# A position MLP whose y term is added once per two rows, and whose sums are stored every four rows

## The chip, the core and the metric

The kernel runs on one core of a Trainium2 chip. The metric is the device time of one execution in microseconds (us). Its engines are TensorE (PE; its weight loads are listed as PEld), VectorE (DVE), ScalarE (ACT), GpSimd (POOL) and SyncE (SP), which here only issues DMAs. Each has a queue of its own and they meet through semaphores. TensorE writes into PSUM, eight banks of 512 fp32 columns on 128 partitions.

## What is computed

The program is a chain of four attention-like layers. The change lies in the first one, a deformable attention, in the MLP that turns relative positions into a bias of the scores:

```python
pos  = grid_q[:, :, None, :] - grid_kv[:, None, :, :]     # 16 groups, 1024 queries, 64 keys, (x, y)
bias = sign(pos) * log1p(abs(pos))
bias = relu(bias @ cpb_w1 + cpb_b1)                       # 2 -> 128
bias = relu(bias @ cpb_w2 + cpb_b2)                       # 128 -> 128
bias = (bias @ cpb_w3 + cpb_b3)                           # 128 -> 1
sim  = q @ k^T + bias;  attn = softmax(sim);  out = attn @ v
```

That is 16 x 1024 x 64 = 1.05 million positions through a 128 x 128 layer.

## The kernel before

The program is a sequence of stages, each a block in which every engine has its own hand-written list of instructions; a block ends with a barrier. The bias stage, `stage_bias`, computes the whole MLP. It goes over 16 groups (bg) of 32 query rows (y), 512 rows in all; two rows are a pair, numbered i (256 pairs, n = i mod 16 within the group). A row has 32 x 64 = 2048 positions, that is four PSUM banks (q = 0 to 3).

- **Layer one** (DVE). The x part with bias and the y part of the hidden value are two tables of fp16 high and low words. DVE takes the maximum of the x table and one row of y values (line 888, 2.29 us a row) into `hw[i % 3]`, three buffers of a pair each, and counts `h1`. Since relu(x + y) = max(x, -y) + y, what is left is a term of y alone, which layer two adds.
- **Layer two** (TensorE). The y term is a product of 12 rows (bf16 pieces of y) with the y weights, line 851. For a row these are four matmuls on four row groups of the array, each into its own bank; they open the banks (start) and are called a y set here. Then for each bank three products in fp16 words (W2 high with low word, W2 low with high, W2 high with high), each as two matmuls of 64 columns side by side, line 862: 24 matmuls a row.
- **Relu** (ACT, line 927): each bank is read out, half of the hidden features into `tops[i % 3]`, half into `bots[i % 2]`, counted as `relu`.
- **Fold** (DVE, line 770): top + ratio x bottom for a pair, 2.35 us, so that layer three has one input instead of two. DVE folds pair i - 3 between the two h1 rows of pair i.
- **Layer three** (TensorE, line 764): for pair i four fp32 matmuls with 32 weight columns side by side, into the bank `p3`. The weight slice puts a pair's two rows in rows of their own, so 16 pairs add up in one bank. TensorE does two pairs of layer three behind every second pair: behind pair i (even) those of i - 2 and i - 1.
- **Copy and store**: once per group ACT adds the bias b3 and copies the bank (line 776), and SP stores it with 4 DMAs of 64 KB (line 781) to `bias_scratch` in DRAM.
- **Tables of the next group**: SP loads coordinates (line 166); ACT computes a value and its high word (lines 904 to 914), DVE the low word (line 874); four such jobs in a group.

The banks of layer two are a ring of seven; layer three has the eighth. At the stage's end SP issues eight loads of 256 KB (line 838), the bias of the first units of the attention stage. The attention stage starts with the last fold, copy and store of the bias stage.

Of the kernel before, what the change touches and what calls it, by code (L numbers as in the profile page):

```python
# [22 lines left out]
P = 128  # L23
# [195 lines left out]
def stage_front(K, sb, ps):  # L219
# [14 lines left out]
    small, x_in, zero = K.sem("small_loaded"), [K.sem(f"x_loaded{i}") for i in range(BLK)], K.sem("front_zeroed")  # L234
# [102 lines left out]
def stage_samples(K, sb, ps):  # L337
# [35 lines left out]
    nx_dram, nt_in, part = K.sem("nx_stored"), K.sem("nt_loaded"), K.sem("samples_step")  # L373
# [3 lines left out]
    cw_in, cw, w_mm, tab_out = K.sem("cpb_w_loaded"), K.sem("cpb_w_step"), K.sem("cpb_w_mm"), K.sem("tab_stored")  # L377
# [4 lines left out]
    with nc.Block() as block:  # L382
        @block.sync
        def _(sp):
            sp.dma_start(w2raw, d["cpb_w2"]).then_inc(cw_in, 16)
            sp.wait_ge(gelu_tanh, 2)
            for axis in range(2):
                for h in range(HALF):
                    sp.dma_start(dn[axis, :, h].unsqueeze(0), off[0:1, axis, h * BLK:(h + 1) * BLK]).then_inc(nx_dram, 16)
            sp.wait_ge(nx_dram, 16 * 2 * HALF)  # L390
            for r in range(QT):
                sp.dma_start(nt[r * n_ax:(r + 1) * n_ax, :], dn.rearrange("a k h j -> (a k h) j")).then_inc(nt_in, 16)
            sp.wait_ge(tab, 3)
            for axis in range(2):
                for r in range(QT):
                    at = r * n_ax + axis * BG
                    sp.dma_start(K.dl[axis, :, r * ROWQ:(r + 1) * ROWQ], pos[at:at + BG]).then_inc(tab_out, 16)
            sp.wait_ge(tab_out, 16 * 2 * QT)
            for job in range(2):
                T.load_coords(K, sp, T.co[job % 2], 0, job)  # L400
            sp.wait_ge(tab, 8)
            for r in range(QT):
                at = r * n_ax + BG
                sp.dma_start(K.dyp[:, :, r * ROWQ:(r + 1) * ROWQ].rearrange("g k y j -> g k (y j)"),
                             pieces[at:at + BG].rearrange("g k y j -> g k (y j)")).then_inc(pieces_out, 16)
            sp.wait_ge(pieces_out, 16 * QT)
            sp.wait_ge(T.ones, 1)
            T.load_y_rows(K, sp, T.rows, 0)
            for job in range(2, T.JOBS):
                sp.wait_ge(T.val_done, job - 1)  # L410
                T.load_coords(K, sp, T.co[job % 2], 0, job)

        @block.vector
        def _(dve):
# [20 lines left out]
            def weights_to_rows():  # L435
# [13 lines left out]
                dve.wait_ge(cw_in, 16)  # L449
# [252 lines left out]
def rings(n, banks):  # L702


    small = next(k for k in range(n) if (n - k * (banks - 1)) % banks == 0)
    at, spread = [], [banks] * ((n - small * (banks - 1)) // banks)
    for k in range(small):
        spread.insert((k * (len(spread) + 1)) // small, banks - 1)
    for size in spread:
        at += range(size)  # L710
    return at


def stage_bias(K, sb, ps):
# [18 lines left out]
    br = T.co[1][:, 0:BANK]  # L733
    banks = [ps(f"l2_ps{i}", [P, BANK]) for i in range(7)]
    p3 = ps("l3_ps", [P, BANK])
    PER = H * CH
    BANK_OF = rings(PER, len(banks))
    NROWS = BG * H

# [5 lines left out]
    def freed_by(row):  # L745
        least = 0
        for c in range(row * CH, row * CH + CH):
            before = [m for m in range(max(0, c - 2 * len(banks)), c) if BANK_OF[m % PER] == BANK_OF[c % PER]]
            if before:
                least = max(least, before[-1] + 1)  # L750
        return least
# [3 lines left out]
    folded, l3, copied, stored = K.sem("relu2_folded"), K.sem("l3_mm"), K.sem("rows_copied"), K.sem("rows_stored")  # L755

    def layer_three(pe, i):
        bg, n = divmod(i, PER_BG)
        pe.wait_ge(folded, i + 1)
        if bg and n == 0:  # L760
            pe.wait_ge(copied, bg)
        for q in range(CH):
            r, u = divmod(q, 2)
            last = nc.tensor.matmul(p3[32 * q:32 * q + 32, :], K.W3[:, 30 - 2 * n:62 - 2 * n], tops[i % 3][:, r, BANK * u:BANK * (u + 1)],  # L764
                                    start=(n == 0), stop=(n == PER_BG - 1), tile_position=(0, 32 * q))
        last.then_inc(l3, 1)
# [5 lines left out]
    def copy_rows(act, bg):  # L772
        act.wait_ge(l3, PER_BG * (bg + 1))
        if bg:
            act.wait_ge(stored, 16 * CH * bg)
        nc.scalar.activation(br, p3[:], ACT.Identity, bias=K.v("cpb_b3")).then_inc(copied, 1)

    def store(sp, bg):
        sp.wait_ge(copied, bg + 1)
        for q in range(CH):  # L780
            sp.dma_start(K.db[bg].rearrange("(i r u a x) j -> r u i a (x j)", r=2, u=2, a=2, x=W // CH)[q // 2, q % 2],
                         br[32 * q:32 * q + 32]).then_inc(stored, 16)
# [5 lines left out]
    def last_rows_summed(pe):  # L788
        layer_three(pe, DBL - 2)
        layer_three(pe, DBL - 1)  # L790

    def last_rows_copied(act):
        copy_rows(act, BG - 1)

    def last_rows_stored(sp):
        store(sp, BG - 1)
        return stored, 16 * CH * BG
# [6 lines left out]
    with nc.Block() as block:  # L804
# [6 lines left out]
        def _(sp):  # L811
# [4 lines left out]
            def y_rows(bg):  # L816
                if bg >= 2:
                    sp.wait_ge(y_mm, H * (bg - 1))
# [14 lines left out]
            sp.wait_ge(stored, 16 * CH * (BG - 2))  # L833
# [7 lines left out]
        def _(pe):  # L841
            for row in range(NROWS):
                bg, y = divmod(row, H)
                i, r = divmod(row, 2)
                out = [banks[BANK_OF[c % PER]] for c in range(row * CH, row * CH + CH)]
                if y == 0:
                    pe.wait_ge(y_in[bg % 2], 16 * 3 * CH * (bg // 2 + 1))
                if freed_by(row):
                    pe.wait_ge(relu, freed_by(row))
                for q in range(CH):  # L850
                    last = nc.tensor.matmul(out[q][:], K.WYD[32 * q:32 * q + YROWS, q % 2], yr[bg % 2][32 * q:32 * q + YROWS, y]  # L851
                                            .unsqueeze(1).to_broadcast([YROWS, W // CH, J]),
                                            start=True, stop=False, tile_position=(32 * q, 0))
                last.then_inc(y_mm, 1)
                pe.wait_ge(h1, row + 1)
                for q in range(CH):
                    u, d = divmod(q, 2)
                    half = slice(d * DH, (d + 1) * DH)
                    h = [hi_lo(hw[i % 3][:, r, BANK * (2 * u + a):BANK * (2 * u + a + 1)]) for a in range(2)]
                    for w, k, stop in ((K.W2H, 1, False), (K.W2L, 1, False), (K.W2H, 0, True)):  # L860
                        for a in range(2):
                            last = nc.tensor.matmul(out[q][a * DH:(a + 1) * DH, :], w[:, half], h[a][:, :, k],  # L862
                                                    start=False, stop=stop, tile_position=(0, a * DH))
                    last.then_inc(l2, 1)
                if r and i and i % 2 == 0:
                    layer_three(pe, i - 2)
                    layer_three(pe, i - 1)

        @block.vector
        def _(dve):  # L870
# [5 lines left out]
            for i in range(DBL):  # L876
                bg, n = divmod(i, PER_BG)
                if i >= 3:
                    dve.wait_ge(l2, 2 * CH * (i - 2))
# [10 lines left out]
                if bg and n == 3:  # L890
                    low(bg, 3)
                if bg + 1 < BG and n in (5, 7, 13):
                    low(bg + 1, (5, 7, 13).index(n))
# [4 lines left out]
        def _(act):  # L898
            def high(bg, job):
                a, half = divmod(job, 2)  # L900
                n = JOBS * bg + job
# [5 lines left out]
                else:  # L907
                    nc.scalar.activation(val, co, ACT.Copy, scale=K.WY[:]).then_inc(val_done, 1)
                act.wait_ge(val_done, n + 1)
# [6 lines left out]
            for row in range(NROWS):  # L916
                bg, y = divmod(row, H)
                i, r = divmod(row, 2)
                for q in range(CH):
# [7 lines left out]
                    nc.scalar.activation((bots[i % 2] if d else tops[i % 3])[:, r, BANK * u:BANK * (u + 1)], banks[BANK_OF[c % PER]][:], ACT.Relu).then_inc(relu, 1)  # L927
                    if bg and y == 2 and q == 0:
                        copy_rows(act, bg - 1)
                if bg and y == 1:  # L930
                    high(bg, 3)
                if bg + 1 < BG and y in (5, 9, 21):
                    high(bg + 1, (5, 9, 21).index(y))


def stage_attention(K, sb, ps):
# [32 lines left out]
    with nc.Block() as block:  # L969
        @block.sync  # L970
        def _(sp):
# [4 lines left out]
            stored, all_stored = K.last_rows_stored(sp)  # L976
            sp.dma_start(OW, K.dram["out_wT"]).then_inc(ow_in, 16)
            for g in range(len(bi), BLK):
                sp.wait_ge(added, g - len(bi) + 1)
                if g == BLK - 1:  # L980
                    sp.wait_ge(stored, all_stored)
# [1223 lines left out]
```

## Time and profile before

| | us |
|---|---|
| median of 3 runs (2777.29 to 2779.13) | 2777.68 |
| the profiled execution | 2777.56 |
| its span, first to last instruction | 2775.7 |
| bias stage, from 103.0 to the barrier at 1968.0 | 1865 |
| TensorE busy, matmuls (share of the span) | 2693.2 (97%) |
| DVE busy | 2153.3 (78%) |
| ACT busy | 1678.5 (60%) |

A table of shares says who is busy, not who is waited for: that is in the list of waits, and what a busy engine really does is in its order of time. Matmuls are pipelined, so the rows of TensorE are read by the distance of their starts, not by their lengths. The span is cut in stages: front and samples up to 103 us, the bias stage, the attention stage from 1968 to 2016, and the rest. The granted clock of TensorE is 1.00 (2.4 GHz) all through the bias stage after its first 7 us.

### The profile page before, as it was taken

Reading aid. Unit: us, or ns where it says so; the run is one execution under the profiler, and the core shown is the slowest. Engines: PE = TensorE matmul, PEld = TensorE weight load, DVE = VectorE, ACT = ScalarE, POOL = GpSimd, SP = SyncE. Lnnn points to the kernel's source line nnn. Section 1 sums busy time; section 2 is a strip of 40 time slices with the busy share of each in tenths; the row PEclk is TensorE's granted clock in tenths of the full one; section 3 lists DMA queues with packets and bytes.
Section 4 is the critical chain, followed back from the end, with each engine's and each line's share of the span. In section 5 each row is a group of like instructions: output and inputs, shape, how many; then the busy total and the mean of one; then the engine's idle time right before and its main releaser. Section 6 shows DMA issues by size and latency. Waiting matters only on the chain. (4 is left out here: it accounts for less than half of the span.)

```text
span 2775.7 us, 46239 instructions
## 1 busy us (share of the span) xinstructions
PE 2693.2 (97%) x20223; PEld 1364.2 (49%) x20223; DVE 2153.3 (78%) x1390; ACT 1678.5 (60%) x2611; POOL 95.4 (3%) x132
## 2 busy tenths in 40 slices
PE   6799999999999999999999999999899999999898
PEld 3434344344344444344443444344578888787553
DVE  4899999999999999999999999999752221254364
ACT  5777777777777767777677776776632222222244
POOL 3000000000000000000000000000422000000000
PEclk9899999999999999999999999999999999999999
DMA  2100010000000000000000010010500000200001
GB/s 72 57 16 30 9 30 30 16 30 9 30 30 16 30 9 30 30 16 30 9 30 27 19 30 9 30 35 9 171 1 1 0 1 1 87 1 1 0 1 61
DMA packets 38762, 72.27 MB, mean 26 GB/s; under 512 B 21089, under 2 KB 22049, under 8 KB 36897
## 3 DMA queue, kind: packets, MB, share of 16 engines
q1 hardware_dynamic: 38496, 69.19, 7.7%
q8 instruction: 159, 2.61, 0.4%
q14 instruction: 43, 0.34, 0.0%
q0 software_dynamic: 64, 0.13, 0.0%
HBM read 60.45 MB, written 8.86 MB: 25 GB/s over the span
## 5 line engine op out<-in xcount | busy, mean ns | idle before, releaser
L862 PE MATMUL l_ps<-mlp_w,W2H 128*64 128x512 f16 x5472 | 913.4, 392 | 1.7 <-DVE mlp_w L888 1.7
L927 ACT ACTIVATE relu_top<-l_ps 128x512 f32<-128x512 f32 x1024 | 612.3, 598 | 415.3 <-PE l_ps L862 370.6
L927 ACT ACTIVATE relu_bottom<-l_ps 128x512 f32<-128x512 f32 x1024 | 612.8, 598 | 79.2 <-PE l_ps L862 1.4
L770 DVE SCALAR_TENSOR_TENSOR relu_top<-relu_bottom,sign_ratio,relu_top 128x2048 f32<-128x2048 f32 x256 | 601.2, 2348 | 11.9 <-PEq L804 6.1
L862 PE MATMUL l_ps<-mlp_w,W2L 128*64 128x512 f16 x2736 | 536.2, 389 | 0.0
L862 PEld LDWEIGHTS l_ps<-mlp_w,W2H 128*64 128x64 f16 x5472 | 304.2, 108 | 357.4 <-issue 78.3
L862 PE MATMUL l_ps<-h_words,W2H 128*64 128x512 f16 x2720 | 453.1, 392 | 0.0
L888 DVE TENSOR_TENSOR mlp_w<-words_x,XN 128x2048 f32<-128x2048 f32 x172 | 391.4, 2286 | 24.5 <-PE l_ps L862 24.5
L888 DVE TENSOR_TENSOR mlp_w<-XN 128x2048 f32<-128x2048 f32 x170 | 387.0, 2290 | 19.4 <-PE l_ps L862 19.1
L862 PE MATMUL l_ps<-h_words,W2L 128*64 128x512 f16 x1360 | 266.1, 388 | 0.0
L764 PE MATMUL l_ps<-relu_top,W 128*32 128x512 f32 x2048 | 246.5, 598 | 0.0
L862 PEld LDWEIGHTS l_ps<-h_words,W2H 128*64 128x64 f16 x2720 | 151.0, 108 | 176.2 <-issue 38.3
L862 PEld LDWEIGHTS l_ps<-mlp_w,W2L 128*64 128x64 f16 x2736 | 153.1, 109 | 120.1 <-issue 0.8
L888 DVE TENSOR_TENSOR h_words<-XN 128x2048 f32<-128x2048 f32 x86 | 196.7, 2288 | 10.7 <-PE l_ps L862 10.7
L888 DVE TENSOR_TENSOR h_words<-words_x,XN 128x2048 f32<-128x2048 f32 x84 | 192.1, 2287 | 12.8 <-PE l_ps L862 12.8
L1280 DVE TENSOR_TENSOR KV_diag_r<-mlp_ps,KV_diag_r 128x512 fp32r<-128x512 f32 x43 | 29.7, 692 | 188.5 <-ACT mlp_ps L1262 188.5
L1261 ACT ACTIVATE KV_diag_r<-mlp_ps,vecs 128x512 fp32r<-128x512 f32 x43 | 29.6, 688 | 175.5 <-PE mlp_ps L1230 175.5
L764 PEld LDWEIGHTS l_ps<-relu_top,W 128*32 128x32 f32 x2048 | 53.2, 109 | 131.9 <-issue 129.0
L851 PE MATMUL l_ps<-XN,y_weights_halves 12*128 12x512 bf16 x1024 | 101.3, 385 | 7.8 <-PEq L382 7.8
L862 PEld LDWEIGHTS l_ps<-h_words,W2L 128*64 128x64 f16 x1360 | 76.0, 108 | 59.5
L851 PE MATMUL l_ps<-y_rows,y_weights_halves 12*128 12x512 bf16 x1024 | 101.1, 384 | 0.0
L851 PEld LDWEIGHTS l_ps<-XN,y_weights_halves 12*128 12x128 bf16 x1024 | 25.9, 91 | 143.6 <-issue 139.8
(403 smaller groups left out, 2763.2 us busy)
## 6 DMA issues: line engine op xcount, KB each, us to landing
XN<-pos_table SPq DMA_DIRECT2D x64, 512.0 KB, 3.7
mlp_w<-in_mlp_w SPq DMA_DIRECT2D x8, 1024.0 KB, 9.5
X<-in_x SPq DMA_DIRECT2D x8, 512.0 KB, 7.7
bias_scratch<-XN SPq DMA_DIRECT2D x64, 64.0 KB, 2.0
XN<-bias_scratch SPq DMA_DIRECT2D x16, 256.0 KB, 5.5
out<-Q SPq DMA_DIRECT2D x16, 256.0 KB, 2.1
XN<-y_pieces SPq DMA_DIRECT2D x96, 12.0 KB
y_rows<-y_pieces SPq DMA_DIRECT2D x96, 12.0 KB
```

What stands on the lines that cost most here:

```text
L764: last = nc.tensor.matmul(p3[32 * q:32 * q + 32, :], K.W3[:, 30 - 2 * n:62 - 2 * n], tops[i % 3][:, r, BANK * u:BANK * (u + 1)], start=(n ...
L770: nc.vector.scalar_tensor_tensor(tops[i % 3], bots[i % 2][:], K.RHO[:], tops[i % 3], ALU.mult, ALU.add).then_inc(folded, 1)
L851: last = nc.tensor.matmul(out[q][:], K.WYD[32 * q:32 * q + YROWS, q % 2], yr[bg % 2][32 * q:32 * q + YROWS, y] .unsqueeze(1).to_broadcast( ...
L862: last = nc.tensor.matmul(out[q][a * DH:(a + 1) * DH, :], w[:, half], h[a][:, :, k], start=False, stop=stop, tile_position=(0, a * DH))
L888: nc.vector.tensor_tensor(hw[i % 3][:, r].rearrange("p (m j) -> p m j", j=J), words_x, words_y[:, 2 * n + r].unsqueeze(1).to_broadcast([P, ...
L927: nc.scalar.activation((bots[i % 2] if d else tops[i % 3])[:, r, BANK * u:BANK * (u + 1)], banks[BANK_OF[c % PER]][:], ACT.Relu).then_inc( ...
L1261: nc.scalar.activation(hid[n % SLOTS][0], pa[n % 3][:], ACT.Gelu, bias=K.v("mlp_b1", f))
L1280: nc.vector.tensor_tensor(lo, pa[n % 3][:], hi.bitcast(F32), ALU.subtract).then_inc(lo_done, 1)
```

## The change

In `stage_bias` three things are changed together.

1. **The y term.** TensorE now works by pairs: layer two of the even row first (it opens the banks), then the even row's y set (it closes them, and each of its four matmuls counts `l2`), then at once the odd row's y set (it opens its banks), then layer two of the odd row.
2. **Layer three.** `p3` is gone. Each two pairs (four rows) have a sum of their own, numbered e (128 of them), in the next bank of the even rows' ring. Odd rows have four fixed banks.
3. **Copy and store.** ACT copies every sum (128 instead of 16 copies) into one of two buffers, SP stores each with 4 DMAs of 8 KB. The jobs of the next group's tables move to other pairs, and value and high are partly apart.

DVE may start the even h1 row of a pair as soon as the even row (not the pair) that used the buffer is through. In the stage before, two semaphores are merged into others with the same counts.

```diff
-    banks = [ps(f"l2_ps{i}", [P, BANK]) for i in range(7)]
-    p3 = ps("l3_ps", [P, BANK])
+    first, second = ([ps(f"l2_{name}_ps{i}", [P, BANK]) for i in range(CH)] for name in ("even", "odd"))
...
+    def use_by_row(i, q):
+        return CH * i + max(0, (i - 1) // 2) + q
+    def use_by_sum(e):
+        return CH * (2 * e + 3) + e
+    def layer_three(pe, e):
+        if e < SUMS - 1:
+            pe.wait_ge(*freed[use_by_sum(e) - CH])
+        for m in range(2):
+            i = 2 * e + m
+            pe.wait_ge(folded, i + 1)
...
-    def copy_rows(act, bg):
-        act.wait_ge(l3, PER_BG * (bg + 1))
+    def copy_rows(act, e):
+        act.wait_ge(l3, 2 * e + 2)
...
             for bg in range(BG):
-                if bg + 1 < BG:
-                    for job in range(1, JOBS):
-                        coords(bg + 1, job)
-                if bg + 1 < BG:
-                    store(sp, bg)
-                if bg + 2 < BG:
-                    coords(bg + 2, 0)
-                    y_rows(bg + 2)
+                for k in range(PER_SUMS):
+                    if bg or k:
+                        store(sp, PER_SUMS * bg + k - 1)
+                    if k == 0 and bg and bg + 1 < BG:
+                        coords(bg + 1, 0)
+                        y_rows(bg + 1)
+                    if k in (1, 2, 4) and bg + 1 < BG:
+                        coords(bg + 1, (1, 2, 4).index(k) + 1)
...
+            for i in range(DBL):
+                bg, n = divmod(i, PER_BG)
+                pe.wait_ge(h1, 2 * i + 1)
+                for q in range(CH):
+                    at = use_by_row(i, q)
+                    if at >= CH:
+                        pe.wait_ge(*freed[at - CH])
+                    layer_two(i, 0, q, first[at % CH])
+                if n == 0:
+                    pe.wait_ge(y_in[bg % 2], 16 * 3 * CH * (bg // 2 + 1))
+                for q in range(CH):
+                    y_term(bg, 2 * n, q, first[use_by_row(i, q) % CH]).then_inc(l2, 1)
+                if i:
+                    pe.wait_ge(relu, 2 * CH * i)
+                for q in range(CH):
+                    last = y_term(bg, 2 * n + 1, q, second[q])
+                last.then_inc(y_mm, 1)
+                pe.wait_ge(h1, 2 * i + 2)
+                for q in range(CH):
+                    layer_two(i, 1, q, second[q]).then_inc(l2, 1)
+                if i and i % 2 == 0:
+                    layer_three(pe, i // 2 - 1)
...
                 if i >= 3:
-                    dve.wait_ge(l2, 2 * CH * (i - 2))
+                    dve.wait_ge(l2, 2 * CH * (i - 3) + CH)
...
                 for r in range(2):
                     if i >= 3 and r:
                         fold(dve, i - 3)
+                        dve.wait_ge(l2, 2 * CH * (i - 2))
```

On TensorE, before, from the end of an odd row over an even row to the next y set (`l_ps` is any bank; a square bracket is a wait):

```order
L862 MATMUL l_ps<-mlp_w,W2H 64x512 x2
L851 MATMUL l_ps<-XN,y_weights_halves 128x512 [waits relu2]
L851 MATMUL l_ps<-XN,y_weights_halves 128x512 x3
L862 MATMUL l_ps<-h_words,W2H 64x512 [waits h1_words]
L862 MATMUL l_ps<-h_words,W2H 64x512
L862 MATMUL l_ps<-h_words,W2L 64x512 x2
...
L862 MATMUL l_ps<-h_words,W2H 64x512 x2
L851 MATMUL l_ps<-XN,y_weights_halves 128x512 [waits relu2]
L851 MATMUL l_ps<-XN,y_weights_halves 128x512 x3
```

The same place in the changed kernel, from the last group of an even row to the first of the odd row:

```order
L845 MATMUL l_even_ps<-h_words,W2H 64x512 [waits relu2]
L845 MATMUL l_even_ps<-h_words,W2H 64x512
L845 MATMUL l_even_ps<-h_words,W2L 64x512 x2
L845 MATMUL l_even_ps<-h_words,W2H 64x512 x2
L850 MATMUL l_even_ps<-XN,y_weights_halves 128x512 x4
L850 MATMUL l_odd_ps<-XN,y_weights_halves 128x512 [waits relu2]
L850 MATMUL l_odd_ps<-XN,y_weights_halves 128x512 x3
L845 MATMUL l_odd_ps<-h_words,W2H 64x512 [waits h1_words]
L845 MATMUL l_odd_ps<-h_words,W2H 64x512
```

The two y sets of a pair now stand side by side, and every group of an even row has a wait for its bank.

On SP, before, the last rows ahead of the end of the bias stage (`L838` are the eight loads of the next stage's bias):

```order
L166 DMA XN<-pos_table 128x1024 [waits table_value] x3
L781 DMA bias_scratch<-XN 16x2x512 [waits rows_copied]
L781 DMA bias_scratch<-XN 16x2x512 x3
L838 DMA XN<-bias_scratch 128x8x64 [waits table_words,h1_words,rows_stored]
L838 DMA XN<-bias_scratch 128x8x64 x7
L804 UNCONDITIONAL_BRANCH
```

On SP in the changed kernel, the same place (`L835` are the same eight loads, `L800` is the end of the block):

```order
L778 DMA bias_scratch<-XN 2x2x512 [waits rows_copied]
L778 DMA bias_scratch<-XN 2x2x512 x3
L778 DMA bias_scratch<-XN 2x2x512 [waits rows_copied]
L778 DMA bias_scratch<-XN 2x2x512 x3
L835 DMA XN<-bias_scratch 128x8x64 [waits h1_words,table_words,rows_stored1,rows_stored0]
L835 DMA XN<-bias_scratch 128x8x64 x7
L800 UNCONDITIONAL_BRANCH
```

The eight loads now stand behind the stores of the stage's last group; the last of these waits for the copy of the last sum but one.

## Rows read from the trace of the kernel before

**Rows 1.** Busy time by stretch: PE, PEld, DVE, ACT, POOL, clock, DMA, GB/s.
```profile
950.00:1070.00 120.00, 120.00 (x1060) 48.34 (x1058) 115.76 (x54) 88.67 (x142) 0.00 (x0) 1.00 0.07 22
```

**Rows 2.** Waits of DVE from 230 to 1910 us: total, times, longest.
```profile
DVE mlp_w L888 <- PE l_ps L862: 40.3, 38, 1.1
DVE h_words L888 <- PE l_ps L862: 22.3, 21, 1.1
```

**Rows 3.** Order of time on PE (start, length, group), around layer three.
```profile
1009.98 0.39 PE L862 MATMUL l_ps<-mlp_w,W2L 128*64 128x512 f16 x2
1010.21 0.39 PE L862 MATMUL l_ps<-mlp_w,W2H 128*64 128x512 f16 x2
1010.53 0.40 PE L851 MATMUL l_ps<-y_rows,y_weights_halves 12*128 12x512 bf16 x4
1010.86 0.42 PE L862 MATMUL l_ps<-mlp_w,W2H 128*64 128x512 f16 x2
1011.11 0.39 PE L862 MATMUL l_ps<-mlp_w,W2L 128*64 128x512 f16 x2
...
1013.71 1.92 PE L764 MATMUL l_ps<-relu_top,W 128*32 128x512 f32 x16
1015.56 0.40 PE L851 MATMUL l_ps<-y_rows,y_weights_halves 12*128 12x512 bf16 x4
```

**Rows 4.** Order of time on PEld: layer three and the next y set.
```profile
999.16 0.16 PEld L764 LDWEIGHTS l_ps<-relu_top,W 128*32 128x32 f32 x8 [0.43 <-issue]
999.62 0.13 PEld L764 LDWEIGHTS l_ps<-relu_top,W 128*32 128x32 f32 x4 [0.30 <-issue]
1000.05 0.13 PEld L764 LDWEIGHTS l_ps<-relu_top,W 128*32 128x32 f32 x4 [0.30 <-issue]
1001.02 0.10 PEld L851 LDWEIGHTS l_ps<-y_rows,y_weights_halves 12*128 12x128 bf16 x4 [0.84 <-issue]
```

**Rows 5.** Order of time on ACT, the one stretch where it is behind.
```profile
229.16 1.14 ACT L908 ACTIVATE XN<-XN,pos_wy 128x1024 f32<-128x1024 f32 x1
...
231.64 0.60 ACT L927 ACTIVATE relu_top<-l_ps 128x512 f32<-128x512 f32 x1
232.13 0.68 ACT L776 ACTIVATE XN<-l_ps,vecs 128x512 f32<-128x512 f32 x1
232.70 0.60 ACT L927 ACTIVATE relu_bottom<-l_ps 128x512 f32<-128x512 f32 x1
233.18 0.61 ACT L927 ACTIVATE relu_top<-l_ps 128x512 f32<-128x512 f32 x1
```

**Rows 6.** Order of time on DVE: fold, h1, low part, h1.
```profile
1001.80 2.35 DVE L770 SCALAR_TENSOR_TENSOR relu_top<-relu_bottom,sign_ratio,relu_top 128x2048 f32<-128x2048 f32 x1
1004.07 2.29 DVE L888 TENSOR_TENSOR h_words<-words_x,XN 128x2048 f32<-128x2048 f32 x1
1006.27 1.38 DVE L874 TENSOR_TENSOR XN<-XN 128x1024 f16<-128x1024 f32 x1
1007.53 2.28 DVE L888 TENSOR_TENSOR mlp_w<-words_x,XN 128x2048 f32<-128x2048 f32 x1
```

**Rows 7.** SP and ACT at the end of the bias stage; the wait of SP.
```profile
1865.61 7.76 SPq L838 DMA_DIRECT2D XN<-bias_scratch  x8
...
1973.74 0.69 ACT L776 ACTIVATE XN<-l_ps,vecs 128x512 f32<-128x512 f32 x1 [6.04 <-PE l_ps L764]
1974.45 2.44 SPq L781 DMA_DIRECT2D bias_scratch<-XN  x4
...
SPq L804 <- PEq L804: 94.4, 1, 94.4
```

**Rows 8.** TensorE: the wait before 103 us, the stretch after, the first scores.
```profile
PE l_ps L851 <- PEq L382: 7.8, 1, 7.8
...
103.00:106.00 3.00, 1.23 (x8) 0.50 (x10) 2.97 (x2) 0.00 (x0) 1.80 (x1) 0.50 0.01 4
...
1968.01 3.81 PE L998 MATMUL score_ps<-KV_diag,Q 128*128 128x128 f32 x32 [0.95 <-PEq L804]
```

More of the change, by code:

```diff
@@ L699, in _ @@
             last.then_inc(v_mm, 1)
[L702 to L711, printed above, removed]
 def stage_bias(K, sb, ps):
@@ L743, in words_of, with sum_ps @@
         return hi_lo((tab_y if a else tab_x[bg % 2])[:, half * HALFC:(half + 1) * HALFC])
[L745 to L751, printed above, removed]
     ones, l_in, y_in, val_done, hi_done, words = T.ones, T.l_in, T.y_in, T.val_done, T.hi_done, T.words
     h1, y_mm, l2, relu = K.sem("h1_words"), K.sem("y_mm"), K.sem("l2_mm"), K.sem("relu2")
[L755 to L766, printed above, removed]
+    folded, l3, copied, stored = K.sem("relu2_folded"), K.sem("l3_mm"), K.sem("rows_copied"), [K.sem(f"rows_stored{i}") for i in range(2)]
+    freed = []
+    for i in range(DBL):
+        freed += [(relu, 2 * CH * i + q + 1) for q in range(CH)]
+        if i and i % 2 == 0:
+            freed.append((copied, i // 2))
+    def use_by_row(i, q):
+        return CH * i + max(0, (i - 1) // 2) + q
+    def use_by_sum(e):
+        return CH * (2 * e + 3) + e
+    def sum_ps(e):
+        return first[use_by_sum(e) % CH] if e < SUMS - 1 else second[CH - 1]
+    def layer_three(pe, e):
[5 more added lines that the diff above has]
+            for q in range(CH):
+                r, u = divmod(q, 2)
+                last = nc.tensor.matmul(sum_ps(e)[32 * q:32 * q + 32, :], K.W3[:, 30 - 2 * m:62 - 2 * m], tops[i % 3][:, r, BANK * u:BANK * (u + 1)],
+                                        start=(m == 0), stop=(m == 1), tile_position=(0, 32 * q))
+            last.then_inc(l3, 1)
     def fold(dve, i):
@@ L841, in _, with layer_two @@
         def _(pe):
[L842 to L846, printed above, removed]
+            def layer_two(i, r, q, out):
+                u, d = divmod(q, 2)
+                half = slice(d * DH, (d + 1) * DH)
+                h = [hi_lo(hw[i % 3][:, r, BANK * (2 * u + a):BANK * (2 * u + a + 1)]) for a in range(2)]
+                for n, (w, k) in enumerate(((K.W2H, 1), (K.W2L, 1), (K.W2H, 0))):
+                    for a in range(2):
+                        last = nc.tensor.matmul(out[a * DH:(a + 1) * DH, :], w[:, half], h[a][:, :, k],
+                                                start=(r == 0 and n == 0), stop=(r == 1 and n == 2), tile_position=(0, a * DH))
+                return last
@@ L926, in _ @@
                         act.wait_ge(folded, i - 1)
[L927 to L933, printed above, removed]
+                    out = second[q] if r else first[use_by_row(i, q) % CH]
+                    nc.scalar.activation((bots[i % 2] if d else tops[i % 3])[:, r, BANK * u:BANK * (u + 1)], out[:], ACT.Relu).then_inc(relu, 1)
+                if r and i % 2 == 0:
+                    slot = i % PER_BG // 2
+                    if i:
+                        copy_rows(act, i // 2 - 1)
+                    if bg and slot == 0:
+                        value(bg, 3)
+                        high(bg, 3)
+                    if bg + 1 < BG and slot in (1, 2, 4):
+                        value(bg + 1, slot // 2)
+                    if bg + 1 < BG and slot in (1, 3, 5):
+                        high(bg + 1, slot // 2)
 def stage_attention(K, sb, ps):
```

96 lines of the change are left out of this document (44 added, 52 removed).

## The prediction

> **What bounds the kernel now.** I read first the busy time by stretch. In the bias stage (103 to 1968 us, 67% of the span) TensorE is busy for all of 120 us at the full granted clock, DVE for 115.8 and ACT for 88.7 [rows 1]. Two engines are therefore close to the bound, and the waits tell which one leads: TensorE is never idle there, while from 230 to 1910 us DVE waits for layer two on TensorE for 40.3 + 22.3 = 62.6 us [rows 2]. TensorE sets the pace, and DVE stands 3.7% behind it.
>
> A busy TensorE is not a TensorE at its peak, so the third view is its order of time. Layer two is issued in twos (two 64-column halves side by side) 0.23 us apart. From the last two of a row to the y set (four matmuls of 12 rows each, side by side) it takes 0.32 us, from the y set to the next two 0.33, and the first step after a y set is 0.25 instead of 0.23 [rows 3]. Streaming 512 columns at 2.4 GHz is 0.213 us by arithmetic (the fp32 sets of layer three step by 0.43, twice that [rows 4]). So every change between the shapes of matmul costs about 0.1 us in which nothing streams; the weight loads show it too: after a change they start together with the matmul and sat idle before, while inside a run (the eight loads at 999.16) the next weights are already loading [rows 4]. Four rows with their layer three take 999.16 to 1013.71 = 14.55 us [rows 3, 4].
>
> **The change on TensorE, per pair of rows.** The number of matmuls stays; their order changes.
> Inside a pair, before: layer two, y set, layer two: 0.32 + 0.33 = 0.65. After: layer two, y set, second y set, layer two: 0.65 + S, where S is the step between two y sets. No row shows two y sets in a row. The lower bound is 0.215, half a step of layer three; the upper is 0.33, a y set followed by an exposed weight load [rows 3]. I take 0.22: the nearest rows are the layer-three sets, same shape after same shape, whose next weights load behind the running matmuls [rows 4]. Cost 0.22.
> Between pairs with no layer three, before 0.32 + 0.33 + 0.25, after two plain steps of 0.23: gain 0.44.
> Between pairs with layer three: the way from the last layer-three set to the y set is 1001.02 - 1000.05 - 0.43 = 0.54 us [rows 4], then 0.33 to layer two; after, layer three goes to layer two directly, which I price as the same exit, 0.54 (bounds 0.43 with no exposed load, 0.54). Gain 0.33.
> Four rows: 2 x 0.22 - 0.44 - 0.33 = -0.33 us, so 14.55 becomes 14.22, and 128 times this is **-43 us** (with S at 0.33: -15; with S at 0.215 and the exit at 0.43: -58).
>
> The Trainium skill speaks against my S: its page "TensorE: Matmul & The Clock Gate", section "Part 3: Packing small matmuls — row/col tiling", says that a weight load overlaps a matmul in flight only when the row groups differ, and the second y set uses the same four row groups as the first. The same section also lets a load into the background buffer pass. Layer two and three here load behind matmuls that hold all rows, against the narrow rule, but with column tiles, so the trace does not settle it for row tiles.
>
> **What it adds to the other engines.** (a) The waits. Every four-matmul group of an even row now waits for its bank, 4 more waits a pair. In layer three the third set stands behind a wait for the fold; its weights load at 999.62, with the second set, and it starts one step of 0.43 later [rows 4], which is its bare length; a wait that is already met costs nothing.
> (b) ACT gets four even banks at once, since the y set ends all four. Let t = 0 be an even pair's even y set. The banks are ready near 0.43; ACT's pitch when it is behind is 0.48 to 0.49 [rows 5], so the even row is done by 2.4, the odd row by 4.4 (its last bank is ready at 3.5). Layer three runs from 3.37 to 5.3, the copy of the sum ends at 5.9 and the next even row starts at 5.2; it needs the copied bank only for its fourth group, at 7.3. Margin 1.4 us. value and high (2.5 us, [rows 5]) end at 8.4, when the next four banks come at 8.5. The odd banks must be free at the next odd y set, and margin there is 1.9 us. ACT adds 112 copies of 0.57 = 64 us, off the path: four rows then cost it 16 x 0.485 + 0.57 + at most 2.5 = 10.8 of 14.2 us.
> (c) DVE per pair: 2.20 + 2.27 + 2.20 = 6.67, plus four low parts of 1.26 in 16 pairs [rows 6]: 13.97 us per four rows, under 14.22. This is a floor: TensorE can gain at most 0.58 us per four rows, 74 us in all. Around n = 4 and 6 two low parts stand close, 3 pairs cost DVE 22.5 against TensorE's 21.3; the three h1 buffers absorb 1.2 us, and the change lets DVE start a row earlier.
> (d) SP's queue. There are 512 stores of 8 KB instead of 64 of 64 KB; a group of four occupies SP for 2.44 us in every 14, alone. But in the last group SP now stands through all the stores before it issues the eight bias loads of the next stage, and those take it 7.76 us [rows 7]. Before they went out at 1865.6, and SP then waited 94.4 us at the barrier that ends the stage [rows 7], so **SP is a member of that barrier**. Now the last store of the stage belongs to sum 126: with t = 0 at pair 254, the copy starts at 5.4, SP issues 0.7 later (1973.74 to 1974.45 in [rows 7]) for 2.4 us, the loads go from 8.6 to 16.3. TensorE's last matmul starts at 11.1 and the last relu ends near 12.1. The barrier therefore opens **4.2 us later** (bounds 0.8, if eight loads cost 0.55 each like two stores do, and 5).
> (e) TensorE then idles about 5 us instead of 1. After its wait of 7.8 us before 103 the granted clock was 0.50, 1.2 GHz [rows 8]. The scores behind the barrier of 1968 take 3.81 us after a wait of 0.95 [rows 8], and at the half clock could take twice that. I take **+2** (bounds 0 and 4).
> (f) The start: pair 0 has no crossing to lose, **+0.4**. The merged semaphores of the front, and the y rows loaded once more than 90 us ahead of use, cost nothing; their cover is the wait of the whole stage in between.
>
> Sum: 2777.56 (the profiled execution; 1.9 us of it outside its span of 2775.7, and 0.1 under the median of the runs, 2777.68) - 43 + 4.2 + 2 + 0.4 = 2741.2, so **2741 us** for the median.
>
> **The rivals.** *Exposed second y set.* The weights of the second y set load only when the first has streamed, S = 0.33: the gain falls to 15 us, and 15 - 6.6 leaves 2769. For it: nothing in the trace shows same-row-group row tiles overlapping; against it: every other run of one shape does overlap. The page named above would give just this. 12%.
> *DVE or ACT pace some pairs.* For it: DVE has only 0.25 us of slack per four rows. Its price is up to 0.1 us per four rows, 13 us: 2754. Against: the buffers. 8%.
> *Slower: the even y set accumulates in four banks at once.* Before, y sets opened their banks (start) and only layer two and three accumulated, each in one bank at a time. Now the even y set adds into four banks together. If the four were served one after another, the set would take 4 x 0.213 instead of 0.213, +0.64 us a pair, 164 us: 2905. It decides for slower once the even set takes over 0.14 us more (36 / 256). No row shows it, but writing four banks together is at full speed now. 5%.
> *The waits break the preloading* at 0.1 us each, 4.5 more inside runs of one shape per pair: +115 us, 2856. [rows 4] speaks against it. 3%.
>
> **How the numbers follow.** Forecast 72%, the four rivals 12, 8, 5 and 3. The forecast's own range is 2731 (gain 49, tail 2) to 2751; the range takes in both bounds of the two unpriced steps (gain 58: 2726; gain 15: 2769), and with them the pacing case. A measurement of this kernel tells about 0.2% from no change, 5.6 us. Faster by more: 72 + 8 and most of 12, say 0.89; within: 0.03; slower: 0.08.
>
> **What would show it.** Step between two y sets 0.22 us (0.33 for the first rival); layer three to layer two 0.54; four rows 14.2 us; DVE's waits for TensorE in the stage down from 62.6 to some 25 us; no TensorE wait for relu, copies or h1. At the end SP's eight loads right before the barrier, the last relu 4 us before the first score, and perhaps a stretch at 1.2 GHz. The forecast is wrong if four rows stay above 14.4, or if the stage after the bias stage loses more than 8 us.

## The result, and the profile after

| | before | after |
|---|---|---|
| median, us | 2777.84 (2777.29 to 2779.13, 4 runs) | 2743.61 (2742.03 to 2747.46, 4 runs) |
| profiled execution, us | 2777.56 | 2744.96 |
| its span, us | 2775.7 | 2743.2 |

The changed kernel takes 0.9883 of the time before, 95% interval 0.9869 to 0.9896: 34 us less. The forecast was 2741.

The busy time by stretch, columns as in [rows 1], after:

```profile
950.00:1070.00 120.00, 120.00 (x1082) 48.09 (x1080) 118.18 (x56) 83.39 (x151) 0.00 (x0) 1.00 0.07 22
```

TensorE is still busy for all of the 120 us, and DVE has moved up from 115.76 [rows 1] to 118.18: the same work in less time. All waits of DVE from 230 to 1910 us, which were 62.6 us for TensorE [rows 2]:

```profile
DVE relu_top L766 <- ACT relu_bottom L940: 27.2, 46, 0.8
```

DVE waits for TensorE no more, and TensorE has no wait at all from 230 to 1880 us. The order of time on TensorE shows what it now does (L845 is layer two, L850 the y sets, L760 layer three); compare [rows 3]:

```profile
1003.71 0.39 PE L845 MATMUL l_even_ps<-mlp_w,W2L 128*64 128x512 f16 x2
1003.93 0.39 PE L845 MATMUL l_even_ps<-mlp_w,W2H 128*64 128x512 f16 x2
1004.25 0.40 PE L850 MATMUL l_even_ps<-y_rows,y_weights_halves 12*128 12x512 bf16 x4
1004.48 0.39 PE L850 MATMUL l_odd_ps<-y_rows,y_weights_halves 12*128 12x512 bf16 x4
1004.79 0.42 PE L845 MATMUL l_odd_ps<-mlp_w,W2H 128*64 128x512 f16 x2
1005.05 0.40 PE L845 MATMUL l_odd_ps<-mlp_w,W2L 128*64 128x512 f16 x2
...
1007.64 1.92 PE L760 MATMUL l_even_ps<-relu_top,W 128*32 128x512 f32 x16
1009.50 0.42 PE L845 MATMUL l_even_ps<-mlp_w,W2H 128*64 128x512 f16 x2
...
1021.88 1.92 PE L760 MATMUL l_even_ps<-relu_top,W 128*32 128x512 f32 x16
```

The second y set starts 0.23 us after the first, layer two 0.31 after it, and four rows take 1021.88 - 1007.64 = 14.24 us instead of 14.55. The weight loads of the same place, as in [rows 4]:

```profile
1004.25 0.10 PEld L850 LDWEIGHTS l_even_ps<-y_rows,y_weights_halves 12*128 12x128 bf16 x4 [0.43 <-issue]
1004.26 0.10 PEld L850 LDWEIGHTS l_odd_ps<-y_rows,y_weights_halves 12*128 12x128 bf16 x4
1004.79 0.11 PEld L845 LDWEIGHTS l_odd_ps<-mlp_w,W2H 128*64 128x64 f16 x2 [0.42 <-issue]
...
1008.53 0.13 PEld L760 LDWEIGHTS l_even_ps<-relu_top,W 128*32 128x32 f32 x4 [0.30 <-issue]
1009.50 0.11 PEld L845 LDWEIGHTS l_even_ps<-mlp_w,W2H 128*64 128x64 f16 x2 [0.84 <-issue]
```

The weights of the second y set are loaded 0.01 us after those of the first, while the first set streams; at every change of shape the loads sat idle (0.42, 0.84) and start together with the matmul.

At the stage's end SP, ACT and TensorE read as follows (L778 the stores, L835 the eight bias loads, L1017 the scores behind the barrier L800):

```profile
1907.47 16.63 SPq L778 DMA_DIRECT2D bias_scratch<-XN  x8
1924.29 7.99 SPq L835 DMA_DIRECT2D XN<-bias_scratch  x8
...
1927.49 0.67 ACT L940 ACTIVATE relu_bottom<-l_odd_ps 128x512 f32<-128x512 f32 x1
...
1926.82 0.39 PE L845 MATMUL l_odd_ps<-mlp_w,W2H 128*64 128x512 f16 x2
1932.72 6.56 PE L1017 MATMUL score_ps<-KV_diag,Q 128*128 128x128 f32 x32 [5.51 <-PEq L800]
```

The last relu ends at 1928.16 and the scores start at 1932.72, right after SP's loads have been issued (1932.28). The same 32 score matmuls take 6.56 us where they took 3.81 [rows 8]. The stretches around it, columns as in [rows 1]:

```profile
1928.00:1935.00 7.00, 2.28 (x11) 2.31 (x12) 2.28 (x1) 0.15 (x1) 0.00 (x0) 0.76 1.25 211
1935.00:1945.00 10.00, 9.90 (x71) 8.15 (x70) 5.67 (x6) 3.71 (x4) 3.80 (x2) 0.83 0.02 4
```

The granted clock is below 1.00 in both: part of each stretch runs at the lower level, 1.2 GHz, behind the idle 5.5 us.

**Where the 32.6 us of span went** (2775.73 to 2743.15). In the profiled executions the stretch from the start of the bias stage to TensorE's last matmul in it is 38.0 us shorter (1863.6 to 1825.7). From that matmul to the first score it takes 4.6 us more (5.90 instead of 1.34): the last relu ends 0.3 us later behind the matmul, and the barrier opens 4.3 us later behind the relu (4.56 instead of 0.30). From the scores to the end of the span it takes 810.4 instead of 807.7 us, 2.7 more. That is -30.7; the other 1.9 us are ahead of the bias stage, where the change only merges two semaphores. That part looks like scatter: the last block of matmuls ahead of the bias stage (`kv_ps`) starts between 71.3 and 74.6 us in the twelve profiled executions here. Before and after:

```profile
74.30 2.08 PE L685 MATMUL kv_ps<-q_phases,XT 128*128 128x128 f32 x8 [13.11 <-DVE q_phases L540]
```
```profile
72.23 3.99 PE L686 MATMUL kv_ps<-q_phases,XT 128*128 128x128 f32 x17 [13.10 <-DVE q_phases L541]
```

### The profile page after: what moved, and what is told of

The parts are those of the page before. It is cut to its first block and busy times, and to the rows that moved or that the text cites. A ratio compares the mean times of both kernels' runs of the same rounds, so it can differ in the third digit from the quotient of the medians.

```text
span 2743.2 us, 47263 instructions
## 1 busy us (share of the span) xinstructions
PE 2655.1 (97%) x20223; PEld 1355.4 (49%) x20223; DVE 2153.2 (78%) x1390; ACT 1569.5 (57%) x2723; POOL 95.6 (3%) x132
## 5 line engine op out<-in xcount | busy, mean ns | idle before, releaser
L940 ACT ACTIVATE relu_top<-l_even_ps 128x512 f32<-128x512 f32 x512 | 308.2, 602 | 446.3 <-PE l_even_ps L850 446.2
L845 PE MATMUL l_even_ps<-mlp_w,W2H 128*64 128x512 f16 x2736 | 455.2, 391 | 10.1 <-DVE mlp_w L897 10.1
L845 PE MATMUL l_odd_ps<-mlp_w,W2H 128*64 128x512 f16 x2736 | 458.3, 394 | 0.0
L940 ACT ACTIVATE relu_bottom<-l_odd_ps 128x512 f32<-128x512 f32 x512 | 334.7, 654 | 0.0
L940 ACT ACTIVATE relu_top<-l_odd_ps 128x512 f32<-128x512 f32 x512 | 328.2, 641 | 0.0
L940 ACT ACTIVATE relu_bottom<-l_even_ps 128x512 f32<-128x512 f32 x512 | 309.8, 605 | 0.0
L845 PE MATMUL l_odd_ps<-mlp_w,W2L 128*64 128x512 f16 x1368 | 269.3, 391 | 0.0
L845 PE MATMUL l_even_ps<-mlp_w,W2L 128*64 128x512 f16 x1368 | 268.4, 389 | 0.0
L845 PEld LDWEIGHTS l_even_ps<-mlp_w,W2H 128*64 128x64 f16 x2736 | 153.0, 108 | 229.9 <-issue 59.6
L845 PEld LDWEIGHTS l_odd_ps<-mlp_w,W2H 128*64 128x64 f16 x2736 | 151.4, 108 | 214.0 <-issue 71.8
L760 PE MATMUL l_even_ps<-relu_top,W 128*32 128x512 f32 x2032 | 244.5, 598 | 0.1
L845 PE MATMUL l_odd_ps<-h_words,W2H 128*64 128x512 f16 x1360 | 227.8, 394 | 0.0
L845 PE MATMUL l_even_ps<-h_words,W2H 128*64 128x512 f16 x1360 | 225.4, 390 | 0.0
L845 PE MATMUL l_odd_ps<-h_words,W2L 128*64 128x512 f16 x680 | 133.9, 391 | 0.0
L845 PE MATMUL l_even_ps<-h_words,W2L 128*64 128x512 f16 x680 | 133.0, 387 | 0.0
```

Of the source, the lines that this page charges most:

```text
L760: last = nc.tensor.matmul(sum_ps(e)[32 * q:32 * q + 32, :], K.W3[:, 30 - 2 * m:62 - 2 * m], tops[i % 3][:, r, BANK * u:BANK * (u + 1)], st ...
L845: last = nc.tensor.matmul(out[a * DH:(a + 1) * DH, :], w[:, half], h[a][:, :, k], start=(r == 0 and n == 0), stop=(r == 1 and n == 2), til ...
```

## The experiments

All are edits of the changed kernel. "Four rows" is the distance of two layer threes, worked out from all of the trace: the median, and where the distances alternate (experiments 2 and 7) the mean. In the diffs `...` and the remarks in brackets or behind `#` stand for code that is left out.

**1. The y set ahead of each row again.**

```diff
+                for q in range(CH):
+                    pe.wait_ge(*freed[at - CH])            # as before where at >= CH
+                    y_term(bg, 2 * n, q, first[at % CH])
                 pe.wait_ge(h1, 2 * i + 1)
                 for q in range(CH):
-                    pe.wait_ge(*freed[at - CH])
-                    layer_two(i, 0, q, first[at % CH])
-                for q in range(CH):
-                    y_term(...).then_inc(l2, 1)
+                    layer_two(i, 0, q, first[...]).then_inc(l2, 1)
```

> The changed kernel with each row's y set ahead of its own layer two again, and all the rest of the change kept (ring of four, fixed odd banks, sums per four rows, 128 copies, 512 stores, late bias loads). Theory (the gain is in the changes of matmul shape on TensorE): four rows go back from 14.24 to 14.54 us, y set to y set vanishes, layer three to y set 0.545, and the time is 2743.6 + 127 x 0.30 = 2782 us, 4 to 7 us above the kernel before. Rival (the gain comes from the looser buffers and waits of the new banks): four rows stay under 14.4, time under 2765.

Measured: 2889.23 us (2888.22 to 2893.78), ratio 1.0412 [1.0395, 1.0430]; four rows 15.41. No theory had that. The trace says why:

```profile
1000.92 1.92 PE L760 MATMUL l_even_ps<-relu_top,W 128*32 128x512 f32 x16
1002.78 0.39 PE L850 MATMUL l_even_ps<-y_rows,y_weights_halves 12*128 12x512 bf16 x3
1003.66 0.39 PE L850 MATMUL l_even_ps<-y_rows,y_weights_halves 12*128 12x512 bf16 x1 [0.49 <-ACT XN L772]
```

The fourth matmul of the y set needs the bank of the sum, which ACT is only now copying. It starts 0.88 us behind the other three: 14.54 + 0.87 = 15.41. All crossings are as in the kernel before (layer two to y 0.32, y to layer two 0.325, layer three to y 0.54). So the crossings behaved as expected, and one wait came on top. So the new banks need the new order (whether the new order needs the new banks was not run): with a sum in the ring of the even rows, the row behind layer three must begin with layer two, which needs its fourth bank 2 us later.

**2. The same without that wait:** the old order only in the even rows of pairs with even i, whose banks wait for relus alone.

```diff
+                if i % 2 == 0:
+                    # y set, opening the banks; then layer two, closing them
+                else:
+                    # layer two, then the y set, as in the changed kernel
```

> The changed kernel, with the old order of the y set (ahead of the row's layer two, opening the banks) only in the even rows of pairs with even i. The banks of these rows wait for relus alone, never for the copy of a sum, so the wait that spoilt e1_y_old_order (62.0 us for the copied bank) can't come. Per four rows two plain steps are lost: between an odd row and the next even row layer two no longer follows layer two (step 0.225) but a y set stands between (0.322 + 0.315, first step after it 0.26 instead of 0.23), and inside the pair layer two, y, layer two (0.322 + 0.315) replaces layer two, y, y, layer two (0.322 + 0.226 + 0.315). Cost 0.637 + 0.03 - 0.225 - 0.226 = +0.22 us per four rows, 14.24 becomes 14.46, times 127 is +28 us: 2743.6 + 28 = about 2771. The rival, that the order costs more than its crossings (as the 15.41 of e1_y_old_order could be read), expects well over 14.5 per four rows; that crossings aren't what the change saved expects 14.24 and 2744.

Measured: 2772.26 us (2768.41 to 2775.62, 10 runs), ratio 0.9984 [0.9974, 0.9993]; four rows 14.45 on average, in turns 14.43 and 14.47 (14.46 was expected). The order of time has both kinds of row, first the even row with its y set beside the odd one's, then an even row with its y set ahead:

```profile
1010.07 0.40 PE L850 MATMUL l_even_ps<-y_rows,y_weights_halves 12*128 12x512 bf16 x4
1010.30 0.39 PE L850 MATMUL l_odd_ps<-y_rows,y_weights_halves 12*128 12x512 bf16 x4
1010.62 0.42 PE L845 MATMUL l_odd_ps<-h_words,W2H 128*64 128x512 f16 x2
...
1013.51 0.39 PE L850 MATMUL l_even_ps<-y_rows,y_weights_halves 12*128 12x512 bf16 x4
1013.83 0.42 PE L845 MATMUL l_even_ps<-mlp_w,W2H 128*64 128x512 f16 x2
```

TensorE has no wait in the stage, as the theory wanted. Moving one y set in four costs 0.21 us per four rows, 29 us in all. Of the change's 0.30 us per four rows 0.09 is left, some 11 us in the stage, less the 7 us that its end costs in the changed kernel: about 4 us. Measured against the kernel before, run beside it (2777.64), it is 5.4 by the medians and 4.4 by the ratio. So the order of the y sets is what the gain is made of, at the price of the crossings.

**3. The eight bias loads behind the fourth store of the last group.**

```diff
                     if k in (1, 2, 4) and bg + 1 < BG:
                         coords(bg + 1, (1, 2, 4).index(k) + 1)
+                    if bg == BG - 1 and k == 3:
+                        bias_loads()
-            (the waits and the eight loads, at the end of SP's list)
```

> The changed kernel with the eight bias loads of the next stage issued behind the fourth store of the last group, as soon as their own waits are met, instead of behind all stores. Theory (SP holds the barrier, and the idle TensorE loses its clock): the last relu is again 0.3 us before the first score (4.26 us gained), the 32 scores take 3.8 us instead of 6.56 (about 2.8 us gained), so 2743.6 - 7 = 2736.5 us. Rival (the barrier only moves work that is hidden behind DVE and POOL in the attention stage): under 3 us gained, 2741 or more. Rival (loads among the last stores delay the copies): slower than 2743.6.

Measured: 2737.87 us (2737.32 to 2739.46), ratio 0.9863 [0.9848, 0.9878]; four rows 14.24.

```profile
1926.33 0.67 ACT L944 ACTIVATE relu_bottom<-l_odd_ps 128x512 f32<-128x512 f32 x1
...
1927.31 3.81 PE L1021 MATMUL score_ps<-KV_diag,Q 128*128 128x128 f32 x32 [1.25 <-PEq L800]
```

The barrier opens 0.31 us after the last relu and the scores take 3.81 us again, both as before the change: 7.0 us less at this place, 5.7 less in the medians. The profiled execution doesn't show the 2.75 us of the scores in its total: from the scores to the end it takes 810.4 us, as long as the changed kernel, since it falls behind the kernel before again further on (by 1.3 us in the attention stage and about 1.5 in the last 12 us of the span). That of experiment 8, with the same loads, takes 807.8, and the kernel before 807.7. This version beats both kernels; its slowest run (2739.46) is below the fastest of the changed kernel (2742.03).

**4. Fewer waits** in the even rows (one for relus at the row's first group and the one for a copied bank, instead of four).

```diff
-                        pe.wait_ge(*freed[at - CH])
+                        sem, count = freed[at - CH]
+                        if sem is copied:
+                            pe.wait_ge(copied, count)
+                        elif q == 0:
+                            pe.wait_ge(relu, (highest count of the four))
```

> The changed kernel with one wait for relu per even row instead of one per bank; the wait for a copied sum stays at its bank. Theory (a wait that is already met costs nothing): four rows stay at 14.24 us, the time at 2743.6 within 3 us. Rival (waits inside a run of layer two hold up the next weights, and make the slower steps of 0.23 to 0.24 us in the odd row behind a layer three): four rows 14.20, about 5 us less, 2738.5.

Measured: 2743.68 us (2741.64 to 2747.82), ratio 0.9885 [0.9870, 0.9899]; four rows 14.24. Waits that are already met are free here.

**5. One increment of four** behind the even y set instead of four of one.

```diff
-                    y_term(bg, 2 * n, q, first[...]).then_inc(l2, 1)
+                    last = y_term(bg, 2 * n, q, first[...])
+                last.then_inc(l2, CH)
```

> The changed kernel with one increment by four on the last of the four matmuls of the even y set, instead of one on each. Theory: increments lie off the path, four rows 14.24, 2743.6 within 3 us. Rival (four increments at once delay what follows, the odd row's first steps of 0.261 and 0.237 instead of 0.252 and 0.227): the odd row falls from 2.57 to 2.53 us, four rows 14.20, about 5 us less.

Measured: 2744.39 us (2743.47 to 2747.01), ratio 0.9887 [0.9872, 0.9902]; four rows 14.24, y set to y set 0.226 as with four increments.

**6. Filler matmuls** on TensorE in the wait for the barrier.

```diff
+            pe.wait_ge(relu, 2 * CH * (DBL - 1) + CH)
+            for k in range(6):
+                layer_two(DBL - 1, k % 2, 0, first[k // 2])
```

> The changed kernel, with 18 pairs of layer-two matmuls more on TensorE behind the last pair (their results are used by nobody), which fill some 4.1 of the 5.5 us in which TensorE waits for the barrier. The barrier stays 4.3 us late, since SP's loads set it. If the idle time of TensorE is what makes the scores longer (6.56 us against 3.81), they take 3.8 to 4.0 again and the rest follows: about -2.8 us, 2741. If the scores are longer for another reason (the loads just ended, or their place against the clock), they stay at 6.5 and the time at 2743.6.

Measured: 2743.18 us (2741.51 to 2744.18), ratio 0.9878 [0.9863, 0.9892]. In the trace:

```profile
1935.03 3.81 PE L1020 MATMUL score_ps<-KV_diag,Q 128*128 128x128 f32 x32 [1.58 <-PEq L800]
...
1928.00:1935.00 7.00, 5.45 (x48) 2.48 (x44) 0.00 (x0) 2.31 (x5) 0.00 (x0) 1.00 1.07 223
1935.00:1945.00 10.00, 9.43 (x80) 7.72 (x80) 8.29 (x6) 3.03 (x3) 3.62 (x2) 1.00 0.27 49
```

The granted clock stays at 1.00 and the scores take 3.81 us: the idle TensorE was the cause of the 2.75 us. From the scores to the end of the span this execution takes 807.4 us, against 810.4 in the changed kernel. In the medians it shows as 0.4 us (1.4 by the ratios), less than expected: its bias stage begins 2.2 us later in the profile, and a gain of 2.8 us is no larger than that scatter, so the run times can't confirm it.

**7. Layer three over 8 of 512 columns,** to see what is bound next.

```diff
-    nc.tensor.matmul(sum_ps(e)[32 * q:32 * q + 32, :], ...
-                     ... tops[i % 3][:, r, BANK * u:BANK * (u + 1)]
+    nc.tensor.matmul(sum_ps(e)[32 * q:32 * q + 32, 0:8], ...
+                     ... tops[i % 3][:, r, BANK * u:BANK * u + 8]
```

> The changed kernel with layer three over 8 of the 512 columns; the other columns of the sums are not computed, so the output isn't the reference's. It takes about 1.7 us of TensorE's work out of every four rows and leaves DVE's and ACT's work as it is. If DVE is the next bound at 6.67 us a pair and four low parts a group, four rows take 13.97 instead of 14.24, a saving of 34 us: about 2709. If nothing but TensorE mattered, four rows would take about 12.5 and the time would be near 2525. A price of DVE pacing that already counts in the changed kernel would show as waits of TensorE for h1 there, which it doesn't have; here they should appear, some 1.4 us per four rows.

Measured: 2701.36 us (2 runs), ratio 0.9728 [0.9708, 0.9747]. The stretch from 1000 us, columns as in [rows 1], and TensorE's largest wait from 230 to 1840 us (total, times, longest):

```profile
1000.00:1120.00 120.00, 111.91 (x1118) 49.37 (x1114) 120.00 (x57) 86.34 (x157) 0.00 (x0) 0.99 0.07 22
```
```profile
PE l_even_ps L760 <- DVE relu_top L766: 112.0, 101, 1.8
```

Now DVE is busy for all of 120 us and TensorE waits for its folds, 112 us in all or about 1.0 us per four rows. The expectation had the waits at h1 and at 1.4 us; no wait for h1 shows. Four rows take 13.94 us on average (13.97 was worked out from DVE's rows), although layer three's share fell from 1.9 to 0.3 us. DVE's ceiling stands where the prediction put it: 0.3 us per four rows below the changed kernel. The total fell 42 us where 34 was expected; the pace explains 38, and the rest wasn't traced.

**8. The edits of 3, 4 and 5 together** (early loads, fewer waits, one increment).

> The changed kernel with the eight bias loads issued behind the fourth store of the last group, one relu wait instead of three or four per even row, and one increment of four instead of four by one. The first was worth 5.7 us, the other two nothing apart: 2738, and nothing more together. If the waits and increments cost something that was hidden while the barrier was late, it is below 2736.

Measured: 2738.97 us (2734.74 to 2739.87), ratio 0.9860 [0.9845, 0.9875]. No faster than the early loads alone.

**9. Short relus, and 10. short h1 and fold,** from pair 6 on, to find the slow steps that are left.

```diff
-  ... tops[i % 3])[:, r, BANK * u:BANK * (u + 1)], out[:], ACT.Relu)
+  ... tops[i % 3])[:, r, BANK * u:BANK * u + 32], out[:, :32], ACT.Relu)
```
```diff
-  hw[i % 3][:, r] (32 x 64 columns), tops and bots over 1024 columns a row
+  hw[i % 3][:, r] (2 x 64 columns), tops and bots over 64 columns a row
```

> What stays open is why four rows take 14.24 us and not 14.20: a step of two layer-two matmuls takes 0.225 us in places and 0.227 to 0.237 in others, always at the same places of the four rows, in the kernel before too. Of 44 steps per four rows these extras sum to 0.09 us (the four first steps behind another shape, 0.25 to 0.26, not counted). This kernel lets each relu from pair 6 on read only 32 of the 512 columns (the rest of its target keeps older values, so the output isn't the reference's), which takes nearly all of ACT's reading of PSUM away and leaves TensorE's instructions as they are. If ACT's reading disturbs TensorE's writing, the slow steps fall to 0.225 and four rows take about 14.15: 2732. If it is DVE's access or TensorE's own issue, the steps stay and four rows take 14.24: 2743.

> The same question from the other side: from pair 6 on DVE's h1 and fold touch 1/16 of their columns (the rest keeps older values, so the output isn't the reference's), which takes nearly all of DVE's traffic away and leaves TensorE's and ACT's instructions as they are. If DVE's traffic makes the slow steps, they fall to 0.225 and four rows take about 14.15: 2732. If it is ACT's reading or TensorE's own issue, four rows stay at 14.24: 2743. It also shows whether any part of DVE's pace (13.97 us per four rows) counts in the changed kernel: its waits for relus (25.6 us) cost TensorE nothing, so removing the work behind them should give nothing.

Measured: 2743.75 us (ratio 0.9883 [0.9855, 0.9912]) and 2745.53 us (0.9890 [0.9861, 0.9919]), two runs each. The same stretch in both, relus first:

```profile
1000.00:1120.00 120.00, 120.00 (x1082) 48.75 (x1080) 118.15 (x56) 36.38 (x152) 0.00 (x0) 1.00 0.07 22
```
```profile
1000.00:1120.00 120.00, 120.00 (x1084) 48.76 (x1080) 19.56 (x55) 83.40 (x152) 0.00 (x0) 1.00 0.07 22
```

ACT's busy time fell from 83 to 36 us, DVE's from 118 to 20, and four rows stayed at 14.24, with every slow step in its old place (to 0.002 us). Neither engine's traffic slows TensorE here. And with DVE almost idle nothing is gained: in the changed kernel TensorE alone sets the pace.

## Why the prediction was right, step by step

**What bounds the kernel.** Right. TensorE's order of time gave the gain, and DVE stands 1.5% behind now (118.18 of 120).

**The y sets (S).** 0.22 forecast, 0.226 measured at 255 of 256 places (the first, at a granted clock of about 0.5, took 0.297). The choice between 0.22 and 0.33 was made by the nearest shape, a run of one shape after itself, and it held. The page "TensorE: Matmul & The Clock Gate" of the Trainium skill, section "Part 3: Packing small matmuls — row/col tiling", has weight loads overlap with matmuls in flight only where the row groups differ; by that S would have been 0.33 and the time 2769. The trace disagrees for this case: both sets use the same four row groups and their loads start 0.01 us apart. It fits the other sentence of that section, that loads into the background weight buffer are pulled ahead too.

**Between pairs.** Layer three to layer two was priced by the exit to a y set, 0.54; measured 0.542. Layer two over the pair's border takes plain steps of 0.225.

**The sum over four rows.** -0.33 forecast, -0.30 measured (14.54 to 14.24), so -38 us for -43. (128 times -0.33 is -42; the forecast's -43 is a slip of 1 us.) The crossings alone give -0.345: +0.43 inside the pairs, -0.45 and -0.33 between them. What was mis-sized is the row behind a doubled y set, which was taken as unchanged. The odd row of the pair after layer three now takes 2.572 us from first to last step instead of 2.53; the first nine of its eleven steps are 0.261, 0.238, 0.234, 0.229, 0.226, 0.234, 0.228, 0.235, 0.235 us where a plain one is 0.225. Over four rows that is 0.04 us, 5.5 us of the total. Experiments 4, 5, 9 and 10 exclude the waits, the increments, ACT's reading and DVE's traffic as causes. What in TensorE's own issue or loads makes them is open; such steps (0.230 to 0.235) stood in the kernel before as well, in fewer places.

**(a) Waits.** Right: free, by experiment 4.

**(b) ACT.** Right in order and time. From the even y set at 1018.49 the forecast had value and high end at 8.4 and the next banks come at 8.5:

```profile
1023.88 0.69 ACT L772 ACTIVATE XN<-l_even_ps,vecs 128x512 f32<-128x512 f32 x1 [0.94 <-PE l_even_ps L760]
1024.46 1.14 ACT L916 ACTIVATE XN<-XN,pos_wy 128x1024 f32<-128x1024 f32 x1
1025.64 1.36 ACT L926 ACTIVATE XN<-XN 128x1024 f16<-128x1024 f32 x1
1027.01 0.60 ACT L940 ACTIVATE relu_top<-l_even_ps 128x512 f32<-128x512 f32 x1
```

The copy starts at 5.4, high ends at 8.5 and the next relu starts at once. Experiment 1 shows how near the edge this ring is: a margin that was counted for one order of work is gone in the other.

**(c) DVE.** The ceiling of 13.97 was right (13.94). The forecast of what DVE would wait for was wrong: not some 25 us for TensorE but 27.2 for ACT's relus. The amount is what DVE's slack leaves. Why its releaser changed is argued, not shown. ACT now gets the even banks in a burst and ends the odd row 0.3 us later behind TensorE (at the stage's end 1.34 instead of 1.04 us behind the start of the last matmul). And DVE may now start h1 when the even row is through, so it comes to the fold sooner. No run separates the two.

**(d) SP.** 4.2 us forecast, 4.3 measured. The eight loads took 7.99 us after the last store, and the barrier opened behind them. Experiment 3 gave it back.

**(e) The clock.** +2 forecast (0 to 4), 2.75 measured. Experiment 6 shows that TensorE's idle time is the cause, and experiment 3 agrees.

**(f) The start.** +0.4 forecast, nothing measured: the first layer two starts 2.35 us after the stage in both, since it waits for h1 either way.

```profile
103.50 0.64 PE L845 MATMUL l_even_ps<-mlp_w,W2H 128*64 128x512 f16 x2 [10.13 <-DVE mlp_w L897]
```

In the sum: the mechanism was right and the sizes a little off. -43 came out as -38, and +6.6 as +7.3 (4.6 and 2.7), so the measured terms give -31 us where -36 was forecast. The medians differ by 34, nearer to the forecast than the terms are. That part is luck: 1.9 us of it in the profiled executions is scatter ahead of the stage, and the rest was not traced. Of the rivals, the exposed second y set, the even set served bank after bank (y set to the next 0.226, not 0.85) and the broken preloading are refuted by the order of time and experiment 4; DVE's pacing is refuted for this kernel by experiment 10, and true of any that makes TensorE 0.3 us faster still.

## What to carry to other kernels

Where one engine is busy all the time, read the distances of its starts at each change of shape: here each change costs 0.1 us, and putting same shapes side by side was worth nearly what the sum of these distances says (0.30 us per four rows where the crossings alone give 0.345). When a change moves DMA issues behind others on a queue, ask whether that queue is a member of the next barrier: 8 us of issues at the wrong end cost 7 of the 38 us that the stage gained, and moving them is a small edit. And an order and a buffer ring are sized together; undoing one part alone can cost more than the whole change brings (146 us against 34 in experiment 1).

## What the runs showed of the hardware

- A second set of four matmuls on the same four row groups starts 0.226 us after the first, its weights loaded 0.01 us after the first set's, in the changed kernel.
- From a doubled y set to layer two it takes 0.315 us, from a single one 0.325, and the second and third step behind it are 0.235 instead of 0.226 (which was so behind one single set in four, too). The medians by place are the same to 0.002 us in the changed kernel and in experiments 4, 5, 9 and 10, so they don't depend on ACT, DVE, waits or increments.
- Four matmuls that add into four open banks at once (the even y set) lose nothing: the next set starts 0.226 us later, the step of two layer-two matmuls.
- TensorE idle for 5.5 us at the barrier goes with a granted clock of 0.76 from 1928 to 1935 us and 0.83 from 1935 to 1945, and with 32 score matmuls of 6.56 us instead of 3.81; with the filler of experiment 6 it stays at 1.00 and they take 3.81.
- Eight DMA issues of 256 KB took SP 7.6 to 8.1 us in a row: 7.76 in the kernel before, 7.99 in the changed one, 7.61 in experiment 3 and 8.13 in experiment 6, on the path or not.
